# The last stage's second rounding moved to VectorE alone, in a kernel of two gated attention and feed-forward blocks

## The reference, cut to what matters

```python
def _fp8_matmul(x2d, w):
    scale_x = jnp.maximum(jnp.max(jnp.abs(x2d)) / 448.0, 1e-06)
    scale_w = jnp.maximum(jnp.max(jnp.abs(w)) / 448.0, 1e-06)
    x8 = (x2d / scale_x).astype(jnp.float8_e4m3fn)
    w8 = (w / scale_w).astype(jnp.float8_e4m3fn)
    return jnp.matmul(x8.astype(x2d.dtype), w8.astype(x2d.dtype).T) * (scale_x * scale_w)
h = _fp8_matmul(x2d, w_fc)            # 4096 x 256 by 256 x 1024
h = jnp.square(jax.nn.relu(h))
out = _fp8_matmul(h, w_proj)          # 4096 x 1024 by 1024 x 256
x = x + jnp.tanh(g_ffn[1]) * out      # x2d above is layernorm(x)
```

## Time and profile before

| | us |
|---|---|
| median of 3 runs | 1726.04 (1722.77 to 1726.96) |
| the profiled execution | 1723.24 |
| its span | 1721.4 |
| VectorE busy in the span | 1118.5 (65%) |
| POOL busy | 976.0 (57%) |
| TensorE matmul busy | 1180.5 (69%) |
| ScalarE busy | 783.4 (46%) |

### The profile page before, as it was taken

One profiled execution on the slowest core, in us unless ns is written; L12 is line 12 of the kernel. 1 busy time (PEld: TensorE's weight loads), 2 busy tenths in 40 slices (PEclk: granted clock), 3 DMA queues, 4 the chain that ended last, 5 costly groups with the idle time before them and its releaser, 6 DMA issues.

```text
span 1721.4 us, 32567 instructions
## 1 busy us (share of the span) xinstructions
PE 1180.5 (69%) x9122; PEld 780.0 (45%) x9132; DVE 1118.5 (65%) x2682; ACT 783.4 (46%) x1599; POOL 976.0 (57%) x910
## 2 busy tenths in 40 slices
PE   5999996233333399999787877743767777946655
PEld 3566664121221366666555655532444444611323
DVE  6899996666666356665444444443755555868998
ACT  3666664222222266766554554532433333534553
POOL 3343342366666533333377767626888888355665
PEclk9999998555555699999877788875788888979786
DMA  9655554032323699999999999963334443000001
GB/s 214 181 151 149 147 151 121 27 111 108 111 107 111 179 296 304 306 312 287 228 253 235 252 242 246 247 188 44 52 55 55 55 55 55 7 0 0 25 24 49
DMA packets 283470, 247.09 MB, mean 144 GB/s; under 512 B 117584, under 2 KB 270032, under 8 KB 282960
## 3 DMA queue, kind: packets, MB, share of 16 engines
q1 hardware_dynamic: 234192, 169.99, 38.5%
q0 software_dynamic: 49152, 75.53, 20.7%
HBM read 111.93 MB, written 117.77 MB: 133 GB/s over the span
## 4 chain that ended last, share of the span: by engine, by line
DMA 26%; POOL 20%; PE 16%; DVE 15%; issue 14%; SPq 6%; ACT 3%; DVEq 0%; POOLq 0%; ACTq 0%
DMA xs<-V 14%; POOL x L624 11%; DMA arena<-xs 8%; POOL region L676 4%; PE bank L1490 3%; DMA xs<-arena,V 2%; POOL rs L569 2%; PE bank L1566 2%; PE bank L1366 2%; DVE arena L972 2%; PE bank L1352 2%; SPq L512 2%; PE bank L1367 1%; PE bank L1378 1%; SPq L499 1%
## 5 line engine op out<-in xcount | busy, mean ns | idle before, releaser
L624 POOL DMA_INDIRECT x<-ys,idx x256 | 403.1, 1575 | 131.5 <-issue 56.2
L642 POOL DMA_INDIRECT xs<-V x192 | 187.1, 975 | 200.2 <-DMA xs<-V 177.0
L1490 PE MATMUL bank<-arena,region 128*128 128x128 f16 x2496 | 252.3, 245 | 1.7 <-ACT arena L835 0.9
L1566 PE MATMUL bank<-arena 128*128 128x128 f16 x1440 | 147.5, 243 | 103.0 <-DMA arena<-xs 98.1
L835 ACT COPY arena<-bank 128x640 f16<-128x640 f16 x192 | 132.2, 689 | 188.1 <-PE bank L1566 187.3
L1378 PE MATMUL bank<-arena 128*72 128x256 f32 (+1 forms) x768 | 209.7, 414 | 0.5 <-ACT arena L717 0.4
L1490 PEld LDWEIGHTS bank<-arena,region 128*128 (+1 forms) x2496 | 187.1, 111 | 18.1 <-issue 5.0
L1566 PEld LDWEIGHTS bank<-arena 128*128 128x128 f16 x1440 | 98.6, 108 | 111.6 <-DMA arena<-xs 80.1
L567 POOL TENSOR_TENSOR ve<-mv,epsilon 128x1 f32<-128x1 f32 x96 | 39.7, 413 | 190.4 <-DVE mv L913 183.1
L1378 PEld LDWEIGHTS bank<-arena 128*72 128x72 f32 (+1 forms) x768 | 115.7, 156 | 45.7 <-issue 11.4
L983 DVE TENSOR_REDUCE arena<-bank 128x8 f32<-128x512 f32 x192 | 124.0, 675 | 12.5 <-PE bank L1352 11.4
(11 more groups left out here) (202 smaller groups left out, 2641.5 us busy)
## 6 DMA issues: line engine op xcount, KB each, us to landing
ys<-arena SPq DMA_DIRECT2D x96, 512.0 KB
arena<-xs SPq DMA_DIRECT2D x288, 160.0 KB
xs<-idx SPq DMA_DIRECT2D x52, 256.0 KB, 2.4
arena<-in_wpairs SPq DMA_DIRECT2D x32, 256.0 KB, 2.6
arena<-in_wpairs SPq DMA_DIRECT2D x128, 64.0 KB, 2.5
x<-ys,idx POOLq DMA_INDIRECT x256
out<-arena SPq DMA_DIRECT2D x16, 256.0 KB, 2.2
xs<-idx SPq DMA_DIRECT2D x52, 64.0 KB, 2.1
```

The costliest lines, as they stand in the source:

```text
L624: pool.indirect_dma_start(tile_x(t), None, ys[t // HT], bass.IndirectOffsetOnAxis(ap=idx[:, t, k:k + 1], axis=0), compute_op=ALU.add).then ...
L642: pool.indirect_dma_start(xs[t // HT], bass.IndirectOffsetOnAxis(ap=at_row[:, t, n % 8:n % 8 + 1], axis=0), ROW[t % NROW], None).then_inc( ...
L1490: mm = pe.matmul(o, lhs(a, w, k), rhs(a, w, k), start=(n == 0), stop=(n == 3 * KT - 1))
L1566: mm = pe.transpose(tpm[n % 2][:, m, :], RAW[g % 2][q][:, m * P:(m + 1) * P], rcv("ident"))
```

## The change

The rounding of the second pass is done by three VectorE instructions, and POOL does nothing there. The scale of the second rounding goes into relu's scale, so that HS is already on the FP8 scale and the rounding uses constants. CC and UU are bf16: c = max(17 v, 0.375), u = c - v, result = c - u. In the first pass the maximum is taken over four banks at once, in two halves of the eight banks, and chunk 0's last subtraction moves from POOL to VectorE. POOL gets one more all-reduce in the second attention, after step 31, whose result nothing reads. The scales are worked out in another order.

```diff
 FP8_MAX = 448.0
 GRID = float(2 ** 20)
 FLOOR = 1.5 * 2.0 ** 14
+SHORT_GRID = 17.0
+SHORT_FLOOR = 1.5 * 2.0 ** -2
+ROOT_MAX = FP8_MAX ** 0.5
+FGRP = 4
 LAST = (NT, NT + 2)
 LAYERS = ((8, 8), (4, 16))
...
     neghalf = sb("neghalf", [P, 1])
     epsilon = sb("epsilon", [P, 1])
     idx = sb("idx", [P, NT, 8], I32)
-    AM, HM, FS = sb("AM", [P, NT]), sb("HM", [P, NCH * NF]), sb("FS", [P, 24])
+    AM, HM, FS = sb("AM", [P, NT]), sb("HM", [P, NCH * NF // FGRP]), sb("FS", [P, 24])
     st = sb("st", [P, 4, 6])
     mv = sb("mv", [P, 4, 2])
     ve = sb("ve", [P, 4, 1])
...
     ys = [nc.dram_tensor(f"ys{h}", (YROWS, H), F32, kind="Internal").ap() for h in range(NHALF)]
     used[0] = 0
-    R, HS, CC, UU = ([carve([CH]) for _ in range(4)] for _ in range(4))
+    R, HS = ([carve([CH]) for _ in range(4)] for _ in range(2))
+    CC, UU = ([carve([CH], BF16) for _ in range(4)] for _ in range(2))
+    used[0] = 4 * 4 * CH
     YO = [carve([2 * H]) for _ in range(2)]
     CX = [arena[:, n * 2 * CH:(n + 1) * 2 * CH] for n in range(2)]
     UX = [arena[:, n * 2 * CH:(n + 1) * 2 * CH] for n in range(2, 4)]
...
                         if t == -2:
                             pool.wait_ge(F["wam"], 2)
                             pool.partition_all_reduce(FS[:, 4:6], FS[:, 1:3], P, RMAX).then_inc(F["amx"], 1)
+                        if t == NT - 1:
+                            pool.partition_all_reduce(FS[:, 14:15], FS[:, 1:2], P, RMAX).then_inc(F["amx"], 1)
             def gather(first, n):
...
             def rounded_x(c, j):
-                if past(c, 1):
-                    pool.wait_ge(F["sx_ready"], c)
-                    pool.wait_ge(F["c_done"], c + 1)
-                    pool.tensor_tensor(UX[j], UX[j], CX[j], ALU.add).then_inc(F["u_done"], 1)
+                if known(c) and c == 0:
+                    return
+                pool.wait_ge(F["sx_ready"], c)
+                pool.wait_ge(F["c_done"], c + 1)
+                pool.tensor_tensor(UX[j], UX[j], CX[j], ALU.add).then_inc(F["u_done"], 1)
                 pool.wait_ge(F["u_done"], c + 1)
                 pool.tensor_tensor(X8[:, :, bass.ds(c * CH, CH)], UX[j].rearrange("p (k t) -> p k t", k=KT),
                                    CX[j].rearrange("p (k t) -> p k t", k=KT), ALU.subtract).then_inc(F["x8_ready"], 1)
...
             tiles(pool, NCH, rounded_x)
             pool.wait_ge(F["hr"], 1)
             pool.partition_all_reduce(FS[:, 7:8], FS[:, 6:7], P, RMAX).then_inc(F["amx"], 1)
-
-            def rounded(c, j):
-
-                if past(c, 2):
-                    pool.wait_ge(F["y_ready"], (c - 1) * 2)
-                for f in range(NF):
-                    pool.wait_ge(F["hu_done"], c * NF + f + 1)
-                    pool.tensor_tensor(H8[j][:, f, :], UU[f % 4], CC[f % 4], ALU.subtract).then_inc(F["h8_ready"], 1)
-
-            tiles(pool, NCH, rounded)
         @block.scalar
         def _(act):
...
                 for f in range(NF):
                     if past(c, 1) or f >= 4:
                         act.wait_ge(F["hs_ready"], c * NF + f - 3)
-                    act.wait_ge(F["h_ready"], NCH * NF + c * NF + f + 1)
-                    act.activation(R[f % 4], bank[f % 4][:, :], ACT.Relu, scale=FS[:, 16:17]).then_inc(F["r_ready"], 1)
+                    act.wait_ge(F["h_ready"], NCH * NF // FGRP + c * NF + f + 1)
+                    act.activation(R[f % 4], bank[f % 4][:, :], ACT.Relu, scale=FS[:, 22:23]).then_inc(F["r_ready"], 1)
                     if f:
                         square(f - 1)
                 square(NF - 1)
...
             dve.wait_ge(F["am_done"], NT)
             biggest(FS[:, 0:1], AM[:, :], F["am_done"])
-            dve.wait_ge(F["amx"], 2)
+            dve.wait_ge(F["amx"], 3)
             dve.tensor_scalar(FS[:, 8:9], FS[:, 3:4], 1.0 / FP8_MAX, 1e-6, ALU.mult, ALU.max).then_inc(F["ams"], 1)
             dve.wait_ge(F["ams"], 1)
             dve.reciprocal(FS[:, 11:12], FS[:, 8:9]).then_inc(F["ams"], 1)
...
                     dve.wait_ge(F["x8_ready"], c - 1)
                 if known(c) and c == 0:
                     quantise(XF[:, :, 0:CH], FS[:, 11:12], both(CX[j]), both(UX[j]), c, "")
+                    dve.wait_ge(F["u_done"], 1)
+                    dve.tensor_tensor(X8[:, :, 0:CH], both(UX[j]), both(CX[j]), ALU.subtract).then_inc(F["x8_ready"], 1)
                 else:
                     dve.wait_ge(F["abs_ready"], c + 1)
...
             def first_pass(c, j):
                 if not known(c) or c + 1 < NCH:
                     round_x(c + 1, 1 - j)
-                for f in range(NF):
-                    dve.wait_ge(F["h_ready"], c * NF + f + 1)
-                    dve.tensor_reduce(HM[:, bass.ds(c * NF + f, 1)], bank[f % 4][:, :], AX.X, ALU.max).then_inc(F["hm_done"], 1)
+                for half in range(2):
+                    n = 2 * c + half
+                    dve.wait_ge(F["h_ready"], n + 1)
+                    dve.tensor_reduce(HM[:, bass.ds(n, 1)], bank8[:, half * FGRP * CH:(half + 1) * FGRP * CH], AX.X, ALU.max).then_inc(F["hm_done"], 1)
             round_x(0, 0)
             tiles(dve, NCH, first_pass, 2)
-            dve.wait_ge(F["hm_done"], NCH * NF)
+            dve.wait_ge(F["hm_done"], 2 * NCH)
             dve.tensor_reduce(FS[:, 6:7], HM[:, :], AX.X, ALU.max).then_inc(F["hr"], 1)
-            dve.wait_ge(F["amx"], 3)
+            dve.wait_ge(F["amx"], 4)
             dve.tensor_scalar(FS[:, 20:21], FS[:, 7:8], 0.0, FS[:, 16:17], ALU.max, ALU.mult).then_inc(F["ams"], 1)
             dve.wait_ge(F["ams"], 5)
-            dve.tensor_tensor(FS[:, 21:22], FS[:, 20:21], FS[:, 20:21], ALU.mult).then_inc(F["ams"], 1)
+            dve.tensor_scalar(FS[:, 21:22], FS[:, 20:21], 1.0 / ROOT_MAX, 1e-3, ALU.mult, ALU.max).then_inc(F["ams"], 1)
             dve.wait_ge(F["ams"], 6)
-            dve.tensor_scalar(FS[:, 20:21], FS[:, 21:22], 1.0 / FP8_MAX, 1e-6, ALU.mult, ALU.max).then_inc(F["ams"], 1)
+            dve.reciprocal(FS[:, 20:21], FS[:, 21:22]).then_inc(F["ams"], 1)
             dve.wait_ge(F["ams"], 7)
-            dve.reciprocal(FS[:, 21:22], FS[:, 20:21]).then_inc(F["ams"], 1)
-            dve.tensor_scalar(FS[:, 23:24], FS[:, 20:21], FS[:, 10:11], tg[:, 3:4], ALU.mult, ALU.mult).then_inc(F["ams"], 1)
+            dve.tensor_tensor(FS[:, 22:23], FS[:, 20:21], FS[:, 16:17], ALU.mult).then_inc(F["fs"], 1)
+            dve.tensor_scalar(FS[:, 15:16], FS[:, 21:22], FS[:, 21:22], FS[:, 10:11], ALU.mult, ALU.mult).then_inc(F["ams"], 1)
+            dve.wait_ge(F["ams"], 8)
+            dve.tensor_scalar(FS[:, 23:24], FS[:, 15:16], tg[:, 3:4], None, ALU.mult).then_inc(F["ams"], 1)
             dve.wait_ge(F["ams"], 9)
-            dve.tensor_scalar(FS[:, 22:23], FS[:, 21:22], GRID, None, ALU.mult).then_inc(F["fs"], 1)
-            dve.wait_ge(F["fs"], 1)
             def rounding(c, j):
                 for f in range(NF):
                     n = c * NF + f
                     dve.wait_ge(F["hs_ready"], n + 1)
-                    if past(c, 1) or f >= 4:
-                        dve.wait_ge(F["h8_ready"], n - 3)
-                    dve.tensor_scalar(CC[f % 4], HS[f % 4], FS[:, 22:23], FLOOR, ALU.mult, ALU.max).then_inc(F["hc_done"], 1)
+                    dve.tensor_scalar(CC[f % 4], HS[f % 4], SHORT_GRID, SHORT_FLOOR, ALU.mult, ALU.max).then_inc(F["hc_done"], 1)
                     dve.wait_ge(F["hc_done"], n + 1)
-                    dve.scalar_tensor_tensor(UU[f % 4], HS[f % 4], FS[:, 21:22], CC[f % 4],
-                                             ALU.mult, ALU.add).then_inc(F["hu_done"], 1)
+                    dve.tensor_tensor(UU[f % 4], CC[f % 4], HS[f % 4], ALU.subtract).then_inc(F["hu_done"], 1)
+                    if f == 0 and past(c, 2):
+                        dve.wait_ge(F["y_ready"], (c - 1) * 2)
+                    dve.wait_ge(F["hu_done"], n + 1)
+                    dve.tensor_tensor(H8[j][:, f, :], CC[f % 4], UU[f % 4], ALU.subtract).then_inc(F["h8_ready"], 1)
                 if past(c, 1):
                     finish(c - 1, 1 - j)
...
             pe.wait_ge(F["w8_ready"], 4)
-            def hidden(c, f, free):
-
-                if past(c, 1) or f >= 4:
-                    pe.wait_ge(free, c * NF + f - 3)
+            def hidden(c, f, at):
+
                 for k in range(KT):
-                    mm = pe.matmul(bank[f % 4][:, :], WF8[:, k, f * P:(f + 1) * P], X8[:, k, bass.ds(c * CH, CH)],
+                    mm = pe.matmul(bank[at][:, :], WF8[:, k, f * P:(f + 1) * P], X8[:, k, bass.ds(c * CH, CH)],
                                    start=(k == 0), stop=(k == KT - 1))
-                mm.then_inc(F["h_ready"], 1)
+                return mm
             def first_pass(c, j):
                 pe.wait_ge(F["x8_ready"], c + 1)
                 for f in range(NF):
-                    hidden(c, f, F["hm_done"])
+                    if f % FGRP == 0 and past(c, 1):
+                        pe.wait_ge(F["hm_done"], 2 * c + f // FGRP - 1)
```

(9 more changed lines are left out.)

## The result

The changed kernel took 1714.58 us (median of 8 runs, 1706.82 to 1716.71), the kernel before beside it 1724.33 us (8 runs). The ratio is 0.9934 with a 95% interval of 0.9914 to 0.9955: faster by 11.4 us by the ratio (9.7 between the medians), where 20.7 were forecast. The sign was right. The size was about half, and the time lies 1.6 us above the upper end of the range.

The account below looks back on a forecast made before the run. VectorE was taken to bound the second pass, with POOL in its way. Second pass -30.1, scales -0.4, first pass -0.9 and added all-reduce +10.7 gave -20.7 us: 1702.5 profiled, 1705.3 on the runs' scale, range 1689 to 1713.

Parts of the forecast that it names:

- What bounds: Second pass: VectorE sets the pace, and POOL's additions hold up its line 1318, a step taking 2.08 us.
- the second pass (-30.1): Second pass: three VectorE instructions, 1.53 us a step, 106.0 us instead of 136.1, minus 30.1.
- Scales (-0.4): Before ScalarE may start: four dependent small instructions instead of six, 0.18 us each, minus 0.4.
- First pass (-0.9): First pass: earlier start but coarser maxima, last maximum ending at 1572.9 against 1573.75, minus 0.9 us.
- Chunk 0's subtraction: Start of the first pass: moved from POOL to VectorE, X8(0) ready at 1521.9 against 1525.94, minus 4.0 us.
- the loop's term: First pass: maxima, floor, POOL's two instructions and four-bank fill sum to 12.3 us per two chunks, 6.15 a chunk against 5.7.
- the low clock: First pass: TensorE's low clock in two halves, 1.7 us each, gave the upper bound of plus 3.
- The added all-reduce (+10.7): Second attention, after step 31: POOL's change to the all-reduce and back is paid anew, uncovered, plus 10.7 us (10.2 to 11.3).
- The rival that it pays: POOL keeps loaded code, so the added all-reduce saves the later one's load; 1690 to 1693 us, chance 0.12.
- Slower: both do: Second pass: both cheap VectorE instructions run at full time, step 2.07 us, about 1734 us; chance 0.04.
- the two cheap instructions: Second pass: one of them runs at full time, plus 0.27 us a step, 17.3 us, giving 1722.6; chance 0.08.
- TensorE didn't take over: Rival: TensorE's clock stays low through the second pass, 13.7 us a chunk, plus 3, 1708 us; chance 0.08.

Follow-up runs that it names:

- e6: e3 with CC and UU in f32 instead of bf16, so the second rounding has no effect; one run, 1713.30 us.
- e4: The kernel before with one more all-reduce as POOL's last instruction, its result unread; 1731.22 us, ratio 1.0057.
- e7: e3 with the maxima taken bank by bank, chunk 0's subtraction still on VectorE; 1689.12 us, ratio 0.9819.
- e5: e3 with the first pass of the kernel before (single banks, chunk 0's subtraction on POOL); 1696.88 us, ratio 0.9853.
- e3: The changed kernel with an ordinary POOL addition behind its last all-reduce and no all-reduce after step 31; 1697.47 us, ratio 0.9858.
- e2: The changed kernel without the all-reduce after step 31; 1701.17 us, ratio 0.9895.

## Why the prediction was right or wrong

- **What bounds, and the second pass (-30.1): right.** Three instructions at 419, 692 and 425 ns against 430, 690 and 410, a step of 1.52, and 137.96 to 107.88 between the first relu and the last H8: 30.1. The reading that POOL was in VectorE's way is borne out by e6: with f32 tiles and an instruction more, VectorE alone is still 13 us faster than the two together. The mixed subtraction stayed at 692 ns and the pure 16-bit one took 425, as read from the earlier trace rows.
- **Scales (-0.4): right.** From the third all-reduce to the first relu are 1.60 us in both kernels with the old chain (before, e4) and 1.24 or 1.25 in the nine with the new one.
- **First pass (-0.9): wrong sign.** From the scales' all-reduce to the end of the last maximum are 57.45 us before and 58.60 after, +1.15. Chunk 0's subtraction brought the 4.0 that were forecast (3.8, e7 against e5); the four-bank maxima cost 6.2 (e3 against e7) where the forecast gave them 3.1; each is a difference of two single profiles. The step that failed is the loop's term, and in it the fill of the four banks: I summed 12.3 us for two chunks, 2.2 of it for a fill with TensorE at the full clock, and took the low clock as a bound only. The other three terms came out (4.41, 0.76 and 4.87 against 4.42, 0.69 and 4.96). Of the three such fills in the changed kernel one took 2.29 at a clock of 1.00 and two took 3.66 and 3.54 at 0.57 and 0.58; in e3 all three took 3.6 to 3.8. The three rounds came to 40.4 us where 37.2 were followed through, and a faster start and end took 1.2 of that back. The loop was named; that it turned the sign was not.
- **The added all-reduce (+10.7): right.** 10.9 in the profile, 11.7 in timed runs. The rival that it pays is refuted by e2.
- **The step that was missing: the end of POOL's program.** I priced each change between all-reduce and ordinary instructions inside the execution, and costed POOL's emptiness in the second pass at nothing. The kernel before had a change back behind its last all-reduce too (1574.5 to 1581.62, show its start); the change took away the instructions that forced it, and so moved it to the first addition of the next execution, where nothing covers it: +6.5.
- **Sum.** -20.7 with +6.5 for the start and +2.0 for the first pass and scales is -12.2; -11.4 was measured. The two profiles agree once the unchanged part's +5.0 is taken off their -6.7: -11.7. The timed figure has an interval of -14.8 to -7.8, so that it comes this close says little.
- **A rival's sum.** "Slower: both do" was given about 1734. By the forecast's own terms it is 64 x 2.07 + 8.1 = 140.6 us for the second pass, 34.6 above the forecast, so about 1740. It didn't come about.
- **The other rivals.** Neither of the two cheap instructions ran at full time. TensorE didn't take over: 63.38 of 91.00 busy.

What stays open: where in the unchanged part the spread of 11 us comes from. It was not looked into, and no run was made for it. What sets TensorE's clock in a fill of four banks is open too.

## What to carry to other kernels

Taking POOL's elementwise work away can pay even where VectorE must do it itself, if VectorE's instructions take longer beside POOL's: line 1318 took 0.75 alone and 1.64 beside POOL, line 1283 0.69 and 1.20, the maxima from PSUM the same. In the two-input instructions here a 16-bit tile paid only where every operand had 16 bits. On POOL, count the changes between all-reduces and ordinary tensor instructions, 6 us there and 7 back: a "warm-up" between ordinary instructions saves nothing (it cost 10.9 here), a change with nothing in between hides itself under the wait, and the last instruction of the program sets what the next execution starts with. Before making an instruction coarser, look for the loop it sits in: the four-bank maximum lost 6.2 us (60.96 against 54.77) while the next chunk's work waited behind it, and with that work issued earlier the pass was 0.8 to 1.4 under the single-bank one.

## What the runs showed of the hardware that was not expected

- What POOL has loaded outlasts an execution, as far as these runs can tell. A kernel that ends in an all-reduce starts its first tensor addition at 16.6 to 16.8 us (three kernels), one that ends in an ordinary instruction at 10.2 to 10.4 (eight).
- The change of code starts when POOL's older work is done, before the new instruction's wait is met (1507.1 for a wait met at 1513.61), so it can be hidden completely. The last all-reduce of the changed kernel shows the same (1590.9 for a wait met at 1597.78). That it is code that is loaded is a reading; what the traces show is the MODIFY_POOL_CONFIG and the time behind it. The Trainium skill (GPSIMD Engine Reference, Instruction dispatch) gives about 6 us for a first call; 5.49 to 6.15 were seen on each way there where nothing was waited for, not only the first, and 6.7 to 7.8 on each way back.
- Memsets, copies (0 to 9 us in the changed kernel) and indirect DMAs (1174.74 to 1182.08 in the kernel before) of POOL did not pay the way back; the first tensor addition after them did.
